# The last key's share of cross-attention: four four-row matmuls a batch in place of sixteen zero-padded ones

## The reference, cut to what matters

```python
q  = (x @ q_w + q_b)        # 16 heads of 32 channels
kv = (cond @ kv_w + kv_b)   # keys and values of 257 rows
attn = softmax(einsum('bhnd,bhmd->bhnm', q * scale, k))      # 32 tokens x 257 keys a head
out  = einsum('bhnm,bhmd->bhnd', attn, v)                    # sum over the 257 keys
x1   = x + out @ proj_w + proj_b
```

## Time and profile before

| | |
|---|---|
| median of three runs | 3367.22 us (3366.77 to 3368.13) |
| the profiled execution | 3372.43 us |
| its span, first to last instruction | 3370.7 us |
| granted TensorE clock, mean | 0.968 |
| busy: PE, PEld | 3082.7 us (91%), 2252.3 us (67%) |
| busy: DVE, ACT, POOL | 2042.9 us (61%), 1294.2 us (38%), 663.1 us (20%) |

### The profile page before, as it was taken

One profiled execution on the slowest core, in us unless ns is written; L12 is line 12 of the kernel. 1 busy time (PEld: TensorE's weight loads), 2 busy tenths in 40 slices (PEclk: granted clock), 3 DMA queues, 4 the chain that ended last, 5 costly groups with the idle time before them and its releaser, 6 DMA issues. The chain is left out here.

```text
span 3370.7 us, 102238 instructions
## 1 busy us (share of the span) xinstructions
PE 3082.7 (91%) x42226; PEld 2252.3 (67%) x42226; DVE 2042.9 (61%) x4203; ACT 1294.2 (38%) x3296; POOL 663.1 (20%) x515
## 2 busy tenths in 40 slices
PE   6999999999999999999999999999999599799975
PEld 5777777777777777777777777777777365444532
DVE  3333466766676677666666666666666587882323
ACT  3444444444444444444444444444443133222321
POOL 0111111111111112111111111111111377302334
PEclk9999999999999999999999999999999688799988
DMA  4222322222222222222222222222221589545379
GB/s 163 68 84 79 109 84 83 78 96 82 79 78 95 83 79 84 96 82 79 84 98 82 79 82 96 83 82 86 99 79 56 144 249 265 160 138 158 126 245 328
DMA packets 297926, 379.12 MB, mean 112 GB/s; under 512 B 159568, under 2 KB 211408, under 8 KB 296016
## 3 DMA queue, kind: packets, MB, share of 16 engines
q1 hardware_dynamic: 287184, 338.19, 31.3%
q0 software_dynamic: 10240, 33.56, 2.9%
HBM read 258.17 MB, written 189.01 MB: 133 GB/s over the span
## 5 line engine op out<-in xcount | busy, mean ns | idle before, releaser
L117 PE MATMUL ring<-cond_high,wkv_high 128*128 128x342 f32 (+1 forms) x1152 | 402.9, 350 | 31.2 <-DVE cond_low L770 13.7
L580 ACT ACTIVATE k_t<-ring,kvb 128x342 f32<-128x342 f32 (+1 forms) x384 | 209.5, 546 | 417.9 <-PE ring L117 417.9
L117 PE MATMUL ring<-cond_high,wkv_low 128*128 128x342 f32 (+1 forms) x1152 | 368.6, 320 | 0.0
L117 PE MATMUL ring<-cond_low,wkv_high 128*128 128x342 f32 (+1 forms) x1152 | 368.6, 320 | 0.0
L117 PE MATMUL ring<-wkv_high,cond_high 128*128 128x512 f32 x768 | 316.4, 412 | 0.0
L814 DVE TENSOR_REDUCE neg_max<-score 128x4 f32<-128x1028 f32 x128 | 157.3, 1229 | 259.9 <-PE score L919 259.9
L166 DVE TENSOR_TENSOR prod<-coef,deltas 128x64 f32<-128x64 f32 (+30 forms) x248 | 304.4, 1227 | 5.9
L117 PE MATMUL ring<-wkv_high,cond_low 128*128 128x512 f32 x768 | 302.6, 394 | 0.0
L117 PE MATMUL ring<-wkv_low,cond_high 128*128 128x512 f32 x768 | 302.0, 393 | 0.0
L613 ACT ACTIVATE prob<-score,neg_max 128x257 f32<-128x257 f32 x512 | 236.5, 476 | 137.8 <-DVE neg_max L814 137.8
L117 PE MATMUL mix<-experts,xs_t 128*128 x624 | 287.0, 604 | 0.0
(11 more groups left out here) (198 smaller groups left out, 5712.3 us busy)
## 6 DMA issues: line engine op xcount, KB each, us to landing
cond<-cond_t_dram SPq DMA_DIRECT2D x128, 385.5 KB, 3.9
xs<-slot_rows SPq DMA_DIRECT2D x78, 256.0 KB
slot_rows<-ys SPq DMA_DIRECT2D x78, 256.0 KB
x_rows<-x SPq DMA_DIRECT2D x64, 256.0 KB, 2.7
vb_rows<-vgb SPq DMA_DIRECT2D x64, 256.0 KB, 3.0
x_in<-x_dram SPq DMA_DIRECT2D x32, 256.0 KB, 3.6
v_last_s<-v_last_rows SPq DMA_DIRECT2D x512, 0.5 KB
kk_rows<-kk_rows_s SPq DMA_DIRECT2D x32, 256.0 KB, 2.7
```

What stands on the lines that cost most here:

```text
L117: last = pe.matmul(out, lhs_t, rhs, start=start and i == 0, stop=stop and i == len(terms) - 1)
L580: act.activation(k_t[:, group, at:at + n], ring_bank[bank][:, 0:n], ACT.Identity, bias=kvb[:, group:group + 1]).then_inc(ring.free[bank], 1)
```

## The change

The operand of the last key loses its padding. `v_last_s` is 4 rows by 128 columns for each of two buffers, and one transfer brings a batch's 512 values into it, row a being group a. `prob_last_t` is 4 rows by 4 heads by 4 groups by 32 tokens: DVE multiplies the 4x128 probabilities of bank L{b} by the 4x4 identity, spread by broadcast, so that for each head g row a holds its probabilities in the columns of group a and zeros in the columns of the other groups. `attend` first does its 32 matmuls over 128 keys, then four matmuls over 4 rows, one a head g, each 32 columns of weights and 128 moving columns, which add to all four groups at once. The counts that PE waits for become 16 a batch in place of 64. The one transfer of zeros at the start takes them from `prob_t`, which POOL clears in place of the two tiles.

```diff
--- before.py
+++ after.py
@@ -229,11 +229,11 @@
         x1n = q_s[:].rearrange("p g t -> p (g t)")
         k_t = sb("k_t", [P, HG, MU])
         v_s = sb("v_s", [P, 2, 2, D])
-        v_last = sb("v_last_s", [P, 2, HG, P])
+        v_last = sb("v_last_s", [HG, 2, P])
         prob = sb("prob", [P, 2, HG, M])
         kq = prob[:, 1].rearrange("p g m -> p (g m)")[:, 0:HG * BU * 2 * N].rearrange("p (i t) -> p i t", t=2 * N)
         prob_t = sb("prob_t", [P, 2, HG * P])
-        prob_last_t = sb("prob_last_t", [P, P])
+        prob_last_t = sb("prob_last_t", [HG, 4, HG, N])
         neg_max = sb("neg_max", [P, HG])
         sums = sb("sums", [P, HG])
         inv_sums = sb("inv_sums", [P, HG])
@@ -296,7 +296,7 @@
                 sp.wait_ge(v_last_moved, 1)
                 sp.dma_start(v_last_d, v_last_all).then_inc(v_last_stored, 16)
                 sp.wait_ge(masks_ready, 1)
-                sp.dma_start(rows["zeros"], v_last[:].rearrange("p w a n -> p (w a n)")[:, 0:D]).then_inc(v_last_stored, 16)
+                sp.dma_start(rows["zeros"], prob_t[:, 0, :]).then_inc(v_last_stored, 16)
                 sp.wait_ge(v_last_stored, 32)
                 sp.wait_ge(loaded, 16 * len(loads))
 
@@ -307,8 +307,7 @@
                 own.did(pool.memset(minus_half[:], -0.5))
                 own.did(pool.memset(half[:], 0.5))
                 own.did(pool.memset(later[:], 1.0))
-                own.did(pool.memset(v_last[:], 0.0))
-                own.did(pool.memset(prob_last_t[:], 0.0))
+                own.did(pool.memset(prob_t[:, 0, :], 0.0))
                 own.did(pool.memset(whole, 1.0))
                 own.then(pool.memset(ident[:], 0.0))
                 own.then(pool.affine_select(out=ident[:], in_=ident[:], compare_op=ALU.not_equal, fill=1.0, base=0,
@@ -417,9 +416,8 @@
                     ring.wait_full(sp, f"O{b - 2}", u)
                 elif not (isinstance(u, int) and u == 0):
                     ring.wait_full(sp, f"O{b + 2}", u - 1)
-                for a in range(HG):
-                    sp.dma_start(v_last[a:a + 1, b % 2, a, :], v_last_d[bass.ds(u * BU + b, 1), a * P:a * P + P])\
-                        .then_inc(v_last_loaded[b % 2], 16)
+                sp.dma_start(v_last[:, b % 2, :], v_last_d[bass.ds(u * BU + b, 1), :].rearrange("r (a x) -> (r a) x", a=HG))\
+                    .then_inc(v_last_loaded[b % 2], 16)
 
             def store_x1(u):
                 ring.wait_read(sp, "PR", u - 1)
@@ -826,7 +824,10 @@
                     dve.tensor_copy(prob_t[:, 1, :], turned[1][:]).then_inc(prob_t1_ready, 1)
 
                     bank = ring.wait_full(dve, f"L{b}", u)
-                    dve.tensor_copy(prob_last_t[0:HG, :], ring_bank[bank][0:HG, 0:P]).then_inc(ring.free[bank], 1)
+                    dve.tensor_tensor(prob_last_t[:], ring_bank[bank][0:HG, 0:P].rearrange("p (g t) -> p g t", g=4)
+                                      .unsqueeze(2).to_broadcast([HG, 4, HG, N]),
+                                      ident[0:HG, 0:HG].unsqueeze(1).unsqueeze(3).to_broadcast([HG, 4, HG, N]), ALU.mult)\
+                        .then_inc(ring.free[bank], 1)
 
                 maximum(0)
                 normalise(0)
@@ -937,18 +938,21 @@
                     pe.wait_ge(exp_done, (n + 2) * HG)
                 pe.wait_ge(prob_t0_ready, n + 1)
                 pe.wait_ge(prob_t1_ready, n + 1)
-                pe.wait_ge(v_last_loaded[b % 2], (u * 2 + b // 2) * 64 + 64)
+                pe.wait_ge(v_last_loaded[b % 2], (u * 2 + b // 2) * 16 + 16)
                 if b == BU - 1:
                     ring.wait_read(pe, f"L{b}", u)
                 bank, full = bank_of(f"O{b}", u)
 
                 for a in range(HG):
-                    for j in range(3):
+                    for j in range(2):
                         for g in range(HG):
                             head, part = slice(a * P + g * HD, a * P + g * HD + HD), slice(g * HD, g * HD + HD)
-                            lhs_t = v_s[:, b % 2, j, head] if j < 2 else v_last[:, b % 2, a, part]
-                            rhs = prob_t[:, j, head] if j < 2 else prob_last_t[:, part]
-                            last = pe.matmul(bank[part, a * N:a * N + N], lhs_t, rhs, start=(j == 0), stop=(j == 2))
+                            pe.matmul(bank[part, a * N:a * N + N], v_s[:, b % 2, j, head], prob_t[:, j, head],
+                                      start=(a == 0 and j == 0), stop=False)
+                for g in range(HG):
+                    part = slice(g * HD, g * HD + HD)
+                    last = pe.matmul(bank[part, 0:P], v_last[:, b % 2, part],
+                                     prob_last_t[:, g].rearrange("p a t -> p (a t)"), start=False, stop=True)
                 last.then_inc(full, 1)
 
             def grams():
```

## The result

The changed kernel takes 3456.64 us, the median of six runs (3445.45 to 3462.47), against 3367.68 us of the kernel before, also of six runs; the ratio is 1.0255 (95%: 1.0232 to 1.0278). The forecast was 3401 us with a range to 3416. The direction was right and the size was not: +89 us instead of +34. The profiled execution took 3445.45 us, with a span of 3443.7, so the two profiles differ by 73 us. The other 16 of the 89 us are not in the profiles: the profiled execution before lies 5 us above its median, that of the changed kernel is the fastest of its six, 11 us under the median. Its mean granted clock was 0.956, that of the other five 0.952 to 0.954, so they probably had more low clock (0.003 of 3450 us is some 10 us, an estimate); they were not profiled, and this stays open.

A forecast was written before the change was run, and what follows sets the result against it. PE's own stream was taken as the bound: its length and where late instruction blocks stop it. Terms 0.6 + 0.4 + 19.2 + 12.6 + 1.5 = +34.3 us gave 3401 us against the median, range 3364 to 3416.

The forecast's parts named there:

- the last turn's stop: PE's 2.03 us stop in the grams copy behind the loop, expected in each pass instead of 1.29: +19.2 us.
- rival 5: Two late instruction blocks in a row: a further 0.4 us in 26 passes, 3412 us; chance 0.05.
- -22 boundary: The new layout's block boundary 22 entries ahead of the grams (234 - 256), in slow code.
- The clock: Longer stops lower PE's clock, so BT behind the grams takes 1.1 us more in 16 x 5/7 passes: +12.6 us.
- What was absorbed: In 5 of 31 passes PE waits for q_s anyway, so the 0.74 us longer stop in grams costs nothing there.
- The batches: In attend's 128 batches, -0.04 us for b = 0 and 1, +0.05 for 2 and 3: +0.6 us in all.
- DVE, SP, POOL: DVE's longer operation, 54 us, hidden but for +0.4 us in unit 0; SP's fewer issues and POOL's edit 0.
- Behind the loop: The second pass's code moves 128 entries against the blocks: +1.5 us, bounds -5 and +5.
- Rival 1: The stop in the grams grows but the clock stays up: 3389 us; chance 0.24.
- rivals 2 and 3: 2: the stop stays 1.29 us, 3368 us, chance 0.13. 3: block in time or cheap matmuls, 3333 or 3354, chance 0.11.
- rival 4: DVE's cover is too thin, so every batch pays 0.42 us: 3421 us; chance 0.04.
- the full clock term: The upper bound of the low clock behind the grams: 16 x 1.7 = +27 us.

The follow-up runs named there:

- e5: The kernel before with the changed kernel's 4x512 DVE operation added behind each copy of the last key's probabilities, into scratch: 3374.39 us, ratio 1.0016.
- e3: The changed kernel with 53 dummy matmuls in unit 0, placing block boundaries 22 and 278 entries into the grams: 3385.38 us, ratio 1.0054.
- e10: The changed kernel with its new operands on 128 rows, the added ones zero, and 53 dummy matmuls on rotating tiles in unit 0: 3363.69 us, ratio 0.9973.
- e2: The kernel before with 16 dummy matmuls in unit 0, placing its loop against the blocks as in the changed kernel: 3445.31 us, ratio 1.0217.
- e9: The changed kernel, four rows kept, with 48 dummy matmuls on rotating tiles in unit 0: 3388.33 us, ratio 1.0044.
- e12: The kernel before with 64 dummy matmuls on rotating tiles in unit 0, one whole block of 256 entries: 3371.57 us, ratio 1.0001.
- e6: The changed kernel with the last group of key products, K21, moved between the two halves of the grams: 3384.01 us, ratio 1.0044.
- e7: The kernel before with the last group of key products, K21, moved between the two halves of the grams: 3360.16 us, ratio 0.9968.
- e1: The changed kernel with 48 dummy matmuls on one tile in unit 0, placing its loop against the blocks as before the change: 3389.06 us, ratio 1.0055.
- e8: The changed kernel with its new operands on 128 rows, rows 4 to 127 zero, and 48 dummy matmuls on rotating tiles: 3370.70 us, ratio 1.0012.

## Why the prediction was right and wrong

**The stop: cause and place right, size wrong.** "I therefore give each pass the last turn's stop: +0.74 us ... 26 x 0.74 = +19.2" is the step that failed most. The main stop grew from 1.51 to 2.49 us, record to record, +0.98 where +0.74 was set; I had one sample, and it was under the mean. The packets of the queue give the size better than the sample did: behind a crossing that itself had to wait, the next block comes 3.6 to 3.9 us after the last, and the fast code uses 1.17 us of that. The second stop, 0.55 us on average, is what rival 5 gave to the -22 boundary (0.4 us by my estimate): the block asked for there is late at 234. I held it to be an alternative with a chance of 0.05, when nothing kept it from coming on top. Together +1.52 in all 31 passes, +47 us.

**The clock: right in kind, too small.** I took 1.1 us in 16 x 5/7 passes, +12.6 us; how the 16 were counted isn't shown. It fell in 21 of 31 passes, against 5 before, in 6 of them for 6.8 us instead of 3.4, and BT grew by 35.6 us in all; a pass with 3.4 us of low clock behind the grams had BT at 4.5 to 4.8 us, record to record, +1.4 to +1.7, since more of the low stretch now fell on BT. My upper bound of 27 us was worked out from one low stretch a pass.

**What was absorbed: too little.** I let 5 passes absorb 0.74 us each, 3.7 us. The waits for q_s gave back 18.5. Stops, BT and waits together are +64 us, where the terms said 31.8. With the batches they make the 73 us of the profiles; the forecast, which was set against medians, has the 16 us of the first section to miss as well.

**The batches.** +0.6 us was set; the loop shows +9.9. The failed step is "for b = 0 and 1 the scores behind them have the same one, so nothing is added there": all four batches lose, 0.10 us for b = 0 and 1 where -0.04 was set, 0.08 and 0.09 for b = 2 and 3 where +0.05 was set. For b = 0 and 1 the scores did not give back what the change of shape ahead of the new records takes. For b = 2 the eight records and the change of shape were set at 0.28 + 0.09 = 0.37 us; with the same 0.32 us for what was removed they cost 0.40 (1.04 - 0.96 + 0.32), of which the change of shape is 0.13. The bounds of -0.1 to +0.1 us a batch held.

**DVE, SP, POOL: right.** PE waited for L827 once, 1.3 us, and it takes 0.67 us (0.69 estimated):

```profile
L827 DVE TENSOR_TENSOR prob_last_t<-ring,ident x128: 668/669/670, 59.7 to 2678.5; 4x512 f32<-4x512 f32 x128
```

DVE is 45.5 us busier where 54 were set. e5 puts a full extra operation at 5 us. That the cover thins once PE is faster is suggested by e3 and e10 alone. Behind the loop, where +1.5 us was set, the profile gained 1.1.

**Rivals.** Rival 1 is out by the clock in 21 passes, rivals 2 and 3 by the stops of 2.49 us and by e2, rival 4 by e5. The forecast and rival 5 were both true. The mistake is in how they were joined: neither excluded the other, and the range's upper end took only one of them. Joined, 3401 + 0.4 x 31 + 14 (the full clock term) = 3427 us, still 30 us short of the median and 18 of the fastest run: the sizes, taken from one or two stops, and the batches did the rest. The sign was no luck, as the place of the stop and the clock behind it came as forecast.

## What to carry to other kernels

Dense stretches of tiny matmuls can be limited by the arrival of PE's instructions, and then an edit that changes the number of instructions ahead of them, even in a written-out first pass, can move the time by more than the edit is worth: 16 harmless matmuls cost 75 us here, and 5 gained 15, while 64 changed nothing. The sign to look for is idle time that nothing releases, always after the same count of instructions, and a packet of the instruction queue just before its end. Before such an edit is judged, it should be measured at a matched place in the instruction stream, as e9 against e12, and where the edit also shortens the loop, the code behind it has to be matched too; no pair of runs here has that for the change as a whole. A piece of slow code inside the dense stretch made it less sensitive: e6 and e7, at two places, differ from the kernel before by +0.4% and -0.3%. And padding of rows that keeps the tile shape of the neighbours was free here, while dropping it was not.

## What the runs showed of the hardware

- The instruction blocks' period is 256 entries: a shift by 256 (e12) left the time within 0.14% and the stop after 149 pairs, as in e1 and the kernel before, and the two stops of a pass of the changed kernel are 256 entries apart.
- A block is one 16 KB packet of queue q8. PE went on 2.2 to 2.9 us after the packet's start at all 93 stops of the two loops, and in and around the grams packets came no closer than 3.3 us before and 3.4 in the changed kernel. That only about one block is fetched ahead is a reading of this, not a separate test.
- A change of tile shape from 128x32 to 4x32 on PE held the next record back by 0.13 us, where with 128x32 kept it was 0.02 (e8). From the first of the eight four-row records to the next matmul it was 0.35 us before the transposes (b = 2) and 0.24 before the scores (b = 0 and 1).
- After stops of 2.3 to 2.9 us, record to record, the granted clock fell to its lower level (1.2 GHz) in 21 of 31 passes, for 3.4 us or twice that; after stops of 1.2 to 1.9 us, before the change, in 5 of 31. A stop of 2.85 us left it up in one pass; what decides there stays open.
- The Trainium skill ("Runtime: NRT & Kernel Launch", Instruction fetch mechanics) calls the crossing of a block mostly hidden. In slow code that agrees with these traces: before the change a pass has nine or ten crossings, and only the one in the grams stops PE each time. Between two boundaries of grams it cost 2.49 us on average.
